# Attention row maxima: folded by GpSimd and turned by VectorE's block transpose with eight small DMAs, in place of TensorE's transpose

## What is computed

```python
Q = linear(concat([q_in, conv1d(q_in)]), qproj)      # K the same way, V plain
scores = einsum('bhqd,bhkd->bhqk', Q, K) / sqrt(DK)
scores = scores * tau[..., None] + delta[:, :, None, :]
attn = softmax(scores, axis=-1)
out = einsum('bhqk,bhkd->bhqd', attn, V)
x = layernorm(x + linear(out, out_w))
x = layernorm(x + einsum('bsd,od->bso', fp4(x), fp4(weight)) + bias)
```

## Time and profile before

| | |
|---|---|
| median of 3 runs | 1684.84 us (1678.03 to 1687.31) |
| span of the profiled execution | 1668.4 us |
| PE busy | 1626.3 us (97%) |
| DVE busy | 1522.9 us (91%) |
| ACT busy | 1311.3 us (79%) |
| POOL busy | 128.4 us (8%) |
| 1024 unit reduces (L237) on DVE | 1228.0 us, 1222 ns each |
| 2048 `st` matmuls (L924) | 524.7 us |
| 8192 `pv_half` matmuls (L937) | 656.1 us |
| 2048 unit matmuls (L227) | 423.6 us |

### The profile page before, as it was taken

The page is one execution under the profiler, slowest core; times in us unless marked ns, Lnnn a source line. Parts: engine busy times, 40 slices in busy tenths (PEclk is TensorE's granted clock), DMA queues, the critical chain, the costliest instruction groups (busy, mean ns, idle before and its releaser), DMA issues.

```text
span 1668.4 us, 33561 instructions
## 1 busy us (share of the span) xinstructions
PE 1626.3 (97%) x13884; PEld 727.6 (44%) x13884; DVE 1522.9 (91%) x1648; ACT 1311.3 (79%) x2375; POOL 128.4 (8%) x166
## 2 busy tenths in 40 slices
PE   8999998999999999999999999999999999999987
PEld 7766663333333333333333333333333343333466
DVE  5789877999999999999999999999999989898887
ACT  2876737888888888888888888888888876778645
POOL 4222223000000000000000000000010000000100
PEclk9999998999999999999999999999999999999999
DMA  3465426000600060015003300422151001010312
GB/s 113 110 177 157 124 86 122 8 8 9 86 8 8 17 76 8 12 26 70 9 8 41 56 8 8 52 45 53 39 63 30 8 8 40 12 41 10 124 59 89
DMA packets 46960, 84.72 MB, mean 51 GB/s; under 512 B 9116, under 2 KB 21020, under 8 KB 44092
## 3 DMA queue, kind: packets, MB, share of 16 engines
q1 hardware_dynamic: 44952, 82.49, 22.8%
q10 hardware_dynamic: 1856, 0.09, 0.1%
HBM read 51.36 MB, written 30.67 MB: 49 GB/s over the span
## 4 chain that ended last, share of the span: by engine, by line
PE 59%; DVE 24%; issue 1%; ACT 0%; ACTq 0%; POOL 0%; DVEq 0%
PE ps L937 25%; DVE mx L237 20%; PE ps L924 20%; PE ps L227 11%; PE ps L870 1%; DVE stats L1173 1%; PE ps L868 1%; PE ps L244 0%; DVE work L1221 0%; DVE work L1232 0%; PE ps L867 0%; DVE small L1216 0%; DVE mv L1179 0%; DVE scr L1225 0%; DVE work L1229 0%
## 5 line engine op out<-in xcount | busy, mean ns | idle before, releaser
L237 DVE TENSOR_REDUCE mx<-ps 128x2 f32<-128x1024 f32 x1024 | 1228.0, 1222 | 67.9 <-PE ps L227 59.6
L1069 ACT ACTIVATE e<-ps 128x512 f32<-128x512 f32 x2048 | 1109.6, 596 | 220.8 <-PE ps L924 182.7
L937 PE MATMUL ps<-e,v_grp 128*32 128x256 f32 x8192 | 656.1, 392 | 0.3 <-issue 0.3
L924 PE MATMUL ps<-q,k 52*128 52x512 f32 x2048 | 524.7, 499 | 4.1 <-PEq L355 3.8
L227 PE MATMUL ps<-k,q 50*128 50x512 f32 x2048 | 423.6, 405 | 9.5 <-DVE mx L237 6.6
L924 PEld LDWEIGHTS ps<-q,k 52*128 52x128 f32 x2048 | 199.6, 183 | 429.4 <-ACT e L1069 385.9
L937 PEld LDWEIGHTS ps<-e,v_grp 128*32 128x32 f32 x8192 | 161.9, 108 | 354.4 <-issue 204.4
L227 PEld LDWEIGHTS ps<-k,q 50*128 50x128 f32 x2048 | 197.7, 187 | 48.1 <-DVE mx L237 34.3
L684 PE MATMUL ps<-x_p,m_p 128*128 128x512 f32 x576 | 144.2, 404 | 0.0
L525 DVE SCALAR_TENSOR_TENSOR hid<-x_c,dw_w,hid 128x512 f32<-128x512 f32 x128 | 103.7, 860 | 19.0 <-ACT hid L466 19.0
L684 PEld LDWEIGHTS ps<-x_p,m_p 128*128 128x128 f32 x576 | 107.0, 190 | 31.8 <-issue 7.3
(11 more groups left out here) (142 smaller groups left out, 623.5 us busy)
## 6 DMA issues: line engine op xcount, KB each, us to landing
k<-k_parts SPq DMA_DIRECT2D x42, 256.0 KB
q<-q_parts SPq DMA_DIRECT2D x42, 256.0 KB
k_parts<-k_sp SPq DMA_DIRECT2D x16, 512.0 KB, 4.9
q_parts<-q_sp SPq DMA_DIRECT2D x16, 512.0 KB, 3.8
att<-ev SPq DMA_DIRECT2D x32, 256.0 KB
x_c<-in_x_t SPq DMA_DIRECT2D x8, 514.0 KB, 5.3
tau_r<-tau_rows SPq DMA_DIRECT2D x16, 256.0 KB
x_in<-in_x SPq DMA_DIRECT2D x8, 512.0 KB, 3.9
```

The source lines that it names most:

```text
L237: nc.vector.tensor_reduce(mx[:, j % 2, :, jh, qt, kc], ps[:, b0:b0 + 2, :], AX.X, ALU.max).then_inc(s_free, 1)
L924: nc.tensor.matmul(ps[:, st_bank(n), :], k_set[r, g % 2, jh, kt * P:(kt + 1) * P], q_set[r, g % 2, jh, lo:lo + CH], start=True, stop=True) ...
L937: last = nc.tensor.matmul(ps[32 * h:32 * (h + 1), 0, PVW * part:PVW * (part + 1)], v_grp[:, kt, h, :], e[:, x % E_BUFS, h * CH + PVW * par ...
L1069: nc.scalar.activation(e[:, x % E_BUFS, h * CH:(h + 1) * CH], ps[:, st_bank(n), :], ACT.Exp).then_inc(e_ready, 1)
```

## The change

The transpose, its padding and its PSUM copy go, and so does the entry in `items`. `split_max` on GpSimd now folds the partial maxima itself: for each of 8 pairs (query block, head of the half) it waits for the last of the pair's four units, takes two `tensor_scalar` operations on 128x1 columns, waits for them, and takes two more, the second of each also negating: 32 small operations in an iteration. Then high and low part as before. `rows_turn` is now a 32x32 block transpose on VectorE of `nm_pad` (128x32), after unit `DEFER` = 2 of the next iteration. `rows_store` needs eight DMAs of 16 pieces of 128 bytes. `q_set` is laid out by chunk, so each q load of `group_load` becomes one per head (20 DMAs for a group in place of 14). `LEAD` becomes 14; iteration 30 issues its units in the first 20 slots, and `unread` goes. In iteration 30 VectorE does the last `rows_turn` after two `gathered` steps and before the reciprocal of z.

```diff
-GROUP_DMAS = 2 * (2 * TERMS + 1)
+GROUP_DMAS = 2 * (TERMS + HH * TERMS + 1)
-        q_set = sb(top, "q_set", [P, 2, HH, L], F32R)
+        q_set = sb(top, "q_set", [P, 2, NQ, HH, CH], F32R)
-        LEAD = 12
-        DEFER = 3
+        LEAD = 14
+        DEFER = 2
-                if u == DEFER - 1 and j > 0:
-                    items.append((j - 1, "rows"))
-        def row_maxima(dve, s):
-            nc.vector.tensor_reduce(nm[:], mx[:, j % 2].rearrange("p a j q c -> p (a j q) c"), AX.X, ALU.max, negate=True).then_inc(nm_max, 1)
         def split_max(pool, j):
-            pool.wait_ge(nm_max, j + 1)
+            folds = 2 * HH * TT * j
+            for qt, jh in FOLD_ORDER:
+                pool.wait_ge(s_free, unit_at[j, qt, jh, NQ - 1] + 1)
+                for half in range(2):
+                    r, parts = (half * HH + jh) * TT + qt, mx[:, j % 2, half, jh, qt]
+                    nc.gpsimd.tensor_scalar(mn[:, r:r + 1], parts[:, 0:1], parts[:, 1:2], parts[:, 2:3], ALU.max, ALU.max).then_inc(mx_folded, 1)
+                folds += 2
+                pool.wait_ge(mx_folded, folds)
+                for half in range(2):
+                    r, parts = (half * HH + jh) * TT + qt, mx[:, j % 2, half, jh, qt]
+                    nc.gpsimd.tensor_scalar(nm[:, r:r + 1], mn[:, r:r + 1], parts[:, 3:4], -1.0, ALU.max, ALU.mult).then_inc(nm_max, 1)
...
-        def rows_turn(pe, s):
-            pe.wait_ge(nm_ready, j + 1)
-            nc.tensor.transpose(ps[:, s_bank(s), 0:P], nm_pad[:].bitcast(F32), ident_f[:]).then_inc(s_full, 1)
-        def rows_copy(dve, s):
-            nc.vector.tensor_copy(nm_rows[:], ps[0:2 * HG * TT, s_bank(s), 0:P]).then_inc(s_free, 1)
+        def rows_turn(dve, j):
+            dve.wait_ge(nm_ready, j + 1)
+            if j > 0:
+                dve.wait_ge(rows_set, j * ROWS_INC)
+            nc.vector.transpose(nm_rows[:].bitcast(F32), nm_pad[:].bitcast(F32)).then_inc(nm_turned, 1)
         def rows_store(sp, j):
-            for h in range(HG):
-                sp.dma_start(q_set[row:row + 2, g % 2, h % HH, lo:lo + CH].bitcast(F32).rearrange("t (a l) -> t a l", a=TT),
-                             nm_rows[h * 2 * TT:(h + 1) * 2 * TT, :].bitcast(F32)).then_inc(rows_set, 16)
+            for half in range(2):
+                for b in range(P // BLOCK):
+                    sp.dma_start(rows[:, :, BLOCK * b:BLOCK * (b + 1)].bitcast(F32), nm_rows[first:first + BLOCK // 2, :].bitcast(F32)).then_inc(rows_set, 16)
...
-                        if s == len(items) - 1:
-                            pe.wait_ge(s_free, s - 1)
-                            unread(s_bank(s), 4)
-                        slots = SLOTS * 3 // 4 if i == NIT - 2 else SLOTS
+                        slots = SLOTS * 5 // 8 if i == NIT - 2 else SLOTS
-                            if u == UNITS - 1:
-                                row_maxima(dve, s)
+                            if u == DEFER - 1:
+                                rows_turn(dve, j - 1)
```

More of the change, by code:

```diff
@@ L188, in layer_kernel @@
                     items.append((j, O_AT[j, u]))
-        items.append((NIT - 1, "rows"))
-        rows_at = {j: s for s, (j, u) in enumerate(items) if u == "rows"}
+        FOLD_ORDER = [(qt, jh) for qt in range(TT) for jh in range(HH)]
         o_at = {u[1:]: s for s, (j, u) in enumerate(items) if (j, u) in [(k[0], v) for k, v in O_AT.items()]}
-        PER = UNITS + 1
         SLOTS = 2 * KT
@@ L226, in s_unit @@
                 r = rows_of(half, K_S)
-                last = nc.tensor.matmul(ps[:, s_bank(s) + half, :], q_set[r, g % 2, jh, lo + qt * P:lo + (qt + 1) * P],
+                last = nc.tensor.matmul(ps[:, s_bank(s) + half, :], q_set[r, g % 2, j % NQ, jh, qt * P:(qt + 1) * P],
                                         k_set[r, g % 2, jh, kc * CH:(kc + 1) * CH], start=True, stop=True)
@@ L270, in split_max @@
             low(nc.gpsimd, nm_parts[:, :, 1], cols, nm_parts[:, :, 0]).then_inc(nm_ready, 1)
-        def rows_store(sp, j):
-            sp.wait_ge(s_free, rows_at[j] + 1)
-            g, lo = j // NQ, j % NQ * CH
-            for h in range(HG):
-                row = HALF * (h // HH) + ROW_MAX
-                sp.dma_start(q_set[row:row + 2, g % 2, h % HH, lo:lo + CH].bitcast(F32).rearrange("t (a l) -> t a l", a=TT),
-                             nm_rows[h * 2 * TT:(h + 1) * 2 * TT, :].bitcast(F32)).then_inc(rows_set, 16)
+        def rows_turn(dve, j):
[3 more added lines that the diff above has]
+            nc.vector.transpose(nm_rows[:].bitcast(F32), nm_pad[:].bitcast(F32)).then_inc(nm_turned, 1)
+        def rows_store(sp, j):
+            sp.wait_ge(nm_turned, j + 1)
+            g = j // NQ
+            for half in range(2):
+                row = HALF * half + ROW_MAX
+                rows = q_set[row:row + 2, g % 2, j % NQ].rearrange("t j (q l) -> t (j q) l", q=TT)
+                for b in range(P // BLOCK):
+                    first = BLOCK * b + BLOCK // 2 * half
+                    sp.dma_start(rows[:, :, BLOCK * b:BLOCK * (b + 1)].bitcast(F32), nm_rows[first:first + BLOCK // 2, :].bitcast(F32)).then_inc(rows_set, 16)
         early = top.enter_context(ExitStack())
@@ L610, in pre_max @@
                         j, u = items[s]
-                        if u == "rows":
-                            rows_copy(dve, s)
-                            continue
                         max_unit(dve, s)
-                        if u == UNITS - 1:
-                            row_maxima(dve, s)
+                        if u == DEFER - 1 and j > 0:
+                            rows_turn(dve, j - 1)
                 for n in range(NCHUNK):
@@ L712, in pre_scores @@
                     for s in pre_at.get((n, place), ()):
-                        if items[s][1] == "rows":
-                            rows_turn(pe, s)
-                        else:
-                            s_unit(pe, s)
+                        s_unit(pe, s)
                 beta(1, 0)
@@ L876, in loaded @@
                         pe.wait_ge(a_norm, n + 1)
-                    def unread(bank, pairs):
-                        for m in range(pairs):
-                            for half in range(2):
-                                r = rows_of(half, K_S)
-                                nc.tensor.matmul(ps[:, bank + half, :], q_set[r, (NG - 1) % 2, 0, 0:P], k_set[r, (NG - 1) % 2, 0, 0:CH], start=True, stop=True)
                     def s_item(s):
@@ L1012, in _ @@
                                     issued += 1
-                                if i == NIT - 2 and 2 * k + jh == slots:
-                                    s_item(len(items) - 1)
                             if x in PROJECT_AT:
```

78 lines of the change are left out of this document (32 added, 46 removed).

## The result

| | before | after |
|---|---|---|
| median | 1685.64 us (4 runs, 1678.03 to 1687.31) | 1726.07 us (4 runs, 1721.83 to 1728.01) |
| ratio, 95% interval | | 1.0265 [1.0233, 1.0296] |
| span of the profiled execution | 1668.4 us | 1720.0 us |
| an iteration from slot 28 to slot 28, where nothing waits | 40.27 us | 39.93 us |
| iterations 3, 7, 11, 15, 19 and 23 | 40.27 to 40.56 us | 48.05 to 49.64 us |

The iteration times are the distances between the weight loads of `st` in slot 28. They say at once where the time went. The seven iterations with refills grew by 56.0 us together; the other iterations from 1 to 30 shrank by 7.0 us together, and iteration 0 grew by 2.7; with 0.1 for the rest that makes the 51.6 between the spans.

A forecast was written before the change was run, and what follows sets the result against it. TensorE's list of slots was taken as the bound. Gains of 17.7, 1.3 and 0.5 us less costs of 0.1 and 1 made 18.4 us off 1684.8, so 1666.4 us; range 1658 to 1680 us.

The forecast's parts named there:

- What bounds the kernel: All iterations: TensorE's list of slots sets the pace at 1.24 us a slot; VectorE has 3.4 us an iteration in hand.
- The entry from the list: Iterations 1 to 29: without the double slot and transpose slot, 0.61 us less each, 17.7 us in all.
- The loads of chunk 4: Around iteration 31: the loads come sooner relative to TensorE, gaining between 0 and 1.0 us, taken as 0.5.
- GpSimd's fold: GpSimd, each iteration: a group takes 0.6 us; no plain stall, 1 us entered for refill iterations, ends 0 and 11.
- The budget of 6.4 us: Refill iterations: GpSimd's time behind refill c=1 for eight groups and the rest, expected to need 5.6 us.
- GpSimd is late behind the refill: Rival, seven refill iterations: VectorE idles before its transpose, waiting for GpSimd; costs 4 to 11 us, chance 0.15.
- Eight DMAs: Row stores after the transpose: issued in 5.2 us, landed after 6.4 of 8.8 us available, so they cost nothing.
- rows land late: Rival at the `st` of slot 28, all iterations: slow DMA issues stall TensorE; +24 us, 1708 us, chance 0.08.
- The transpose: VectorE: the 128x32 block transpose takes between 0.18 and 0.28 us, taken as 0.18.
- VectorE's part: VectorE loses copy and fold and gains a transpose: 0.3 to 0.4 us less, worth nothing outside iterations 27 to 29.
- The prediction's other price for the fold: Moving the fold from VectorE, where slack hides its 0.22 us, to GpSimd costs between 0 and 11 us.
- From the span to the median: Whole run: the median lies 16.4 us above the profiled span, and this was left as it is.

The follow-up runs named there:

- the kernel with two groups first: The changed kernel with two of GpSimd's eight fold groups ahead of refill c=1 and six behind it: 1690.33 us, ratio 1.007.
- the kernel whose clock was held: The changed kernel with 18 pairs of unread score matmuls, one on each partition half, in slot 22 of refill iterations: 1696.19 us, ratio 1.0088.
- the first try: The changed kernel with 20 unread matmuls on one half of the partitions in slot 22 of each refill iteration: 1719.67 us, ratio 1.0195.

## Why the prediction was wrong

**What bounds the kernel** held: TensorE's list set the pace of plain iterations, and with the copy made small they take 32 x 1.24 = 39.68 us.

**The entry from the list: right in kind, half in size.** I entered 0.61 us an iteration and got 40.27 - 39.93 = 0.34. Of the double slot I had asked what stands late in it, and not what other engines did while it lasted. ScalarE's copy needs 0.60 us there, and 0.31 of that came to light. Over iterations 1 to 30 without the seven the gain was 7.0 us, the 1.74 of iteration 30 included, where 22 x 0.61 + 1.3 = 14.7 had been entered. The loads of chunk 4 brought nothing: iteration 31 went from 50.82 to 50.98.

**GpSimd's fold: the step that failed.** I wrote: "I take for a group of two plus two: 0.20 for the first, 0.07 for the wait, 0.1 for each of the other three: 0.6 us; the bounds are 0.4 and 4 x 0.22 + 0.07 = 0.95." A group took 1.33. Two errors are in that line. The neighbours that I drew on, memsets and copies, have no column operands, which add 0.07 us each; six of them are in a group, 0.45 us. And I let independent operations overlap down to 0.1 us. Even the upper bound left the operands out: the group with constants, 0.83, lies inside it. The rest followed by the working as it stood. The budget of 6.4 us was right: GpSimd needed 417.99 - 406.70 = 11.3, so it was 4.9 late, and the trace has 4.92 on VectorE. Of that 0.57 cost nothing where 0.4 had been entered, so the stall is 4.35 us at full clock; the slot's 5.09 have 0.7 more because its end (1.73 us, and 1.00 in the kernel with two groups first) already ran at the lower clock. In iterations without refills the last group and the rest took 1.94 us, over the bound of 1.75 but inside the 2.48 that there were: of 32 transposes 8 waited.

**What no step held: the clock after a stall.** The rival "GpSimd is late behind the refill" named the mechanism, place and number of iterations, and the sign by which it would show, idle time of VectorE ahead of its transpose in every fourth iteration; its price was 4 to 11 us. With the right price for a group it would have been 7 x (4.9 - 0.4) = 31.5 us in place of 1, and the sum 1684.8 - 19.4 + 31.5 = 1697 us, close to the 1696.2 of the kernel whose clock was held. That closeness is in part luck: the sum has twice the gain that plain iterations had, and nothing for the unread pairs. The other 30 us or so are TensorE at 0.50 after each stall. I priced a stall by its length only. The start of the loop also runs at the lower clock, and moves the time of an execution: iteration 0 took 43.7 us in the profiled execution of before, and 53.5 in that with the fold on VectorE, where the windows have

```profile
262.00:280.00 18.00, 18.00 (x103) 6.10 (x106) 9.07 (x8) 9.34 (x18) 10.64 (x18) 0.50 1.04 160
```

while the kernel with the fold ahead of the refill was granted 0.79 in the same 18 us and took 43.8.

**Eight DMAs: right.** The issues took 5.21 us for 5.2 entered, and in the list of waits no `st` waits for a DMA. The rival that rows land late didn't happen; pieces of 128 bytes cost nothing that is visible here. That pieces under 512 bytes are slower (the Trainium skill, DMA: Bandwidth & Descriptors, Specifications) changed nothing in this place. **The transpose: right**, 0.202 us (median) for 0.18, inside 0.18 to 0.28. **VectorE's part** is a gain that nobody needed, as predicted: with the fold on VectorE plain iterations take 39.99, as with the fold on GpSimd ahead of the refill. The working had one wrong sum there: 0.28 + 0.22 less 0.18 to 0.28 is 0.2 to 0.3 us, not 0.3 to 0.4; outside iterations 27 to 29 nothing hung on it. The prediction's other price for the fold, 0 to 11 us for moving it to GpSimd, came to 59 behind the refill, and to nothing that these runs tell apart ahead of it.

**From the span to the median.** I carried 16.4 us as something that lies around the span. In nearly every execution it is about 1.8 us (1721.83 for a span of 1720.0). By that the profiled execution of before took about 1670.2 us, some 15 less than the median of its other runs. The difference didn't decide the sign. The fold on VectorE shows it best: span 1671.1 with 53.49 us in iteration 0, while its other three runs took 1659.6 to 1660.7.

**What stays open.** Why the clock fell after some stalls of 1.7 us and stayed after others isn't settled: in both TensorE was idle 1.43 us. What the unread matmuls must be like to hold it isn't either: the pairs differ from the first try in the halves that they use and in their number. Nor is it shown why iteration 0 is long in some executions. A kernel with both halves of the plain iteration's gain would need the copy off the bank that PV writes next, so a free PSUM bank; that wasn't tried.

## What to carry to other kernels

Before work goes to an engine that has time to spare on average, find the one iteration where it comes behind something else there, and price it with a row that has the same operands; operations as small as these are nearly all fixed cost (a 128x16 cast took 0.20 us, a 128x1 operation 0.215), and column operands add to it. A stall of TensorE costs its length and what the clock takes afterwards, here about as much again; so let a new wait have a margin, or move the work ahead of what it queues behind, which turned 2.7% slower into 1.0% faster. And before a long slot is counted as gain, look at what every other engine does under it.

## What the runs showed of the hardware

- A 128x1 `tensor_scalar` on GpSimd took 215 ns with constants, 290 with one column operand, 366 with two. Consecutive ones didn't shrink to the 0.03 us of the memsets in the earlier trace rows: two without a wait between them took 0.39 us with constants and 0.70 with two columns each.
- After 4.1 us without work TensorE was granted 0.50 (1.2 GHz) in six cases of six, and three to seven slots took about 2.16 in place of 1.24 us; in iteration 3 that lasted some 12 us. After 1.43 us without work the clock fell in four cases of six, and after 1.57 us, in the kernel before with the fold on GpSimd, in one of six.
- Matmuls on one half of the partitions held the clock in five of seven stalls (it fell in iterations 11 and 23), pairs on both halves in all seven. On one half alone PE's busy time was full whether the clock held or fell.
- A block transpose of 128x32 float32 on VectorE took 0.20 us; eight DMAs of 2 KB in pieces of 128 bytes were issued in 5.21 us, as fast one by one as four of 512-byte rows.
